# Six blocks of a matrix loaded at the beginning of a graph network's gated stage and not at its end

## The reference

```python
h = relu(layernorm(x)); x = x + L0(h)      # 10 propagation steps
h = relu(layernorm(x)); x = x + L1(h)      # the gated layer
h = relu(layernorm(x)); x = x + L2(h)      # two GCN convolutions with residuals
h = relu(layernorm(x)); x = x + L3(h)      # two weighted GCN convolutions, log_softmax

# L1, the gated layer
concat = concatenate([h[src], h[dst], edge_attr])
gated  = sigmoid(concat @ W_e + b_e) * softplus(concat @ W_n + b_n)
h_new  = segment_sum(gated, dst)
return h + h_new / clip(edge_count, 1)
```

## Time and profile before

| | |
|---|---|
| median of 3 runs | 2653.1 us |
| profiled execution | 2654.15 us, its span 2652.3 us |
| PE, DVE, ACT, POOL busy over the span | 85%, 62%, 50%, 42% |
| mean granted TensorE clock | 0.778 |
| gated stage, SP's first issue of it to that of the next stage | 1088.49 to 2148.15 us |
| DMA over the gated stage | some 110 to 120 GB/s in most slices |

### The profile page before, as it was taken

One profiled execution on the slowest core, in us unless ns is written; L12 is line 12 of the kernel. 1 busy time (PEld: TensorE's weight loads), 2 busy tenths in 40 slices (PEclk: granted clock), 3 DMA queues, 4 the chain that ended last, 5 costly groups with the idle time before them and its releaser, 6 DMA issues. The chain is left out here.

```text
span 2652.3 us, 55540 instructions
## 1 busy us (share of the span) xinstructions
PE 2257.7 (85%) x18268; PEld 2117.0 (80%) x18269; DVE 1637.7 (62%) x3208; ACT 1322.6 (50%) x2410; POOL 1109.4 (42%) x1222
## 2 busy tenths in 40 slices
PE   2999998699999999688888888788887768689998
PEld 1888888699999999587777777677777658689998
DVE  7998899764334335575666666656666564465465
ACT  1555555533333332265555555555555532267686
POOL 2666666300000000477777777777777701200000
PEclk6999999899999999655555555555555569879999
DMA  1444434300000001444444444444444551095281
GB/s 55 140 141 144 146 130 146 123 2 2 2 2 2 2 2 31 136 120 115 109 113 115 110 112 116 109 110 118 110 110 117 177 199 46 22 390 212 95 291 31
DMA packets 155980, 281.63 MB, mean 106 GB/s; under 512 B 73475, under 2 KB 123878, under 8 KB 150470
## 3 DMA queue, kind: packets, MB, share of 16 engines
q1 hardware_dynamic: 117158, 200.48, 23.3%
q0 software_dynamic: 38688, 79.28, 11.6%
HBM read 210.52 MB, written 69.15 MB: 105 GB/s over the span
## 5 line engine op out<-in xcount | busy, mean ns | idle before, releaser
L1245 POOL DMA_INDIRECT layer_R<-source_terms,layer_srcs x800 | 780.2, 975 | 243.7 <-issue 243.7
L1477 PE MATMUL layer_zp<-layer_right,layer_left 96*128 96x192 f32 x1342 | 476.9, 541 | 161.5 <-DVE layer_left L1264 158.4
L1477 PEld LDWEIGHTS layer_zp<-layer_right,layer_left 96*128 96x128 f32 x1342 | 409.6, 331 | 178.1 <-DVE layer_left L1264 167.4
L1008 PEld LDWEIGHTS layer_acc<-layer_U,graph_CT 128*128 128x128 f16 x6250 | 524.4, 97 | 32.0 <-ACT layer_U L937 22.5
L1008 PE MATMUL layer_acc<-layer_U,graph_CT 128*128 128x192 f16 (+1 forms) x6250 | 529.5, 246 | 23.4 <-ACT layer_U L937 21.5
L1498 PEld LDWEIGHTS layer_acc<-layer_hot,layer_G 128*98 128x98 f32 x1648 | 272.6, 274 | 108.1 <-DVE layer_aggT L1318 107.8
L1498 PE MATMUL layer_acc<-layer_hot,layer_G 128*98 128x32 f32 x1648 | 288.2, 344 | 45.8 <-DVE layer_aggT L1318 45.8
L2278 PE MATMUL layer_acc<-layer_V,layer_turn 128*128 128x96 f32 x2500 | 288.9, 278 | 0.6 <-issue 0.6
L2278 PEld LDWEIGHTS layer_acc<-layer_V,layer_turn 128*128 128x128 f32 x2500 | 287.0, 195 | 0.9 <-issue 0.9
L1423 ACT ACTIVATE layer_y<-layer_R 128x1152 f32<-128x1152 f32 x135 | 156.3, 1158 | 238.7 <-DVE layer_R L1292 238.7
L1292 DVE TENSOR_TENSOR layer_R<-layer_zp,layer_R 128x1152 f32<-128x1152 f32 x135 | 182.4, 1351 | 146.6 <-DMA layer_R<-source_terms,layer_srcs 146.4
(11 more groups left out here) (316 smaller groups left out, 3125.5 us busy)
## 6 DMA issues: line engine op xcount, KB each, us to landing
layer_ring<-W_blocks SPq DMA_DIRECT2D x41, 1600.0 KB, 7.6
W_blocks<-nodes_x SPq DMA_DIRECT2D x150, 200.0 KB, 1.9
layer_left<-in_attr SPq DMA_DIRECT2D x68, 384.0 KB
C_blocks<-build_Cblk SPq DMA_DIRECT2D x25, 800.0 KB, 3.4
layer_C<-C_blocks SPq DMA_DIRECT2D x19, 800.0 KB, 20.2
layer_R<-source_terms,layer_srcs POOLq DMA_INDIRECT x800
W_blocks<-build_Wtwo SPq DMA_DIRECT2D x50, 200.0 KB, 1.9
layer_rows<-target_rows SPq DMA_DIRECT2D x68, 96.0 KB
```

Of the source, the lines that this page charges most:

```text
L1008: return pe.matmul(acc[:, k % RING, 0:columns], CT[:, t, k * P:(k + 1) * P], pairs[:, cur, t, 0:columns], start=(t == 0), stop=(t == NT - 1))
L1245: nc.gpsimd.indirect_dma_start(R[:, i, u, :], None, P_d, bass.IndirectOffsetOnAxis(ap=at_u, axis=0)).then_inc(s_R[i], 16)
L1477: pe.matmul(out[u], left[:, i, u * P:(u + 1) * P], right[:, i, :], start=(u % 2 == 0), stop=False, skip_group_check=True)
```

## The change

The loop over the six blocks moves from behind the last pair of loads to behind the first one, ahead of the pair for steps 2 and 3. It gets a semaphore of its own, since `s_wa` is waited for early, at the value 144 of the nine weight loads, by DVE and PE. No instruction of another engine changes. Line numbers behind the first edit grow by one (L1193 is L1194 after).

```diff
@@ semaphores of gated_edges
+        s_first = m.sem("first_blocks_loaded")
@@ SP's program
             four_steps(sp, bases, counts, 0)
             loads(0, 0)
+            for j in range(FIRST):
+                sp.dma_start(C_first[:, j, :, :].rearrange("p k d -> p (k d)"), C_d[j, :, :]).then_inc(s_first, 16)
             with sp.Fori(0, NL - 1) as four:
                 loads(1, four * LONG + 2)
...
             loads(1, (NL - 1) * LONG + 2)
-            for j in range(FIRST):
-                sp.dma_start(C_first[:, j, :, :].rearrange("p k d -> p (k d)"), C_d[j, :, :]).then_inc(s_wa, 16)
             for i in range(NS - (NL - 1) * LONG):
                 more_loads(bases[i], counts[i])
-            sp.wait_ge(s_wa, 16 * (2 * LONG + 1 + FIRST))
+            sp.wait_ge(s_first, 16 * FIRST)
```

## The result

The changed kernel takes 2660.53 us (median of 11 runs, 2658.62 to 2662.39), the kernel before 2653.72 in the same comparison (11 runs, 2650.69 to 2655.84). The ratio is 1.0026, 95% interval 1.0017 to 1.0034: 6.8 us slower, where 3.1 were forecast. The median lies 1 us outside the range that was given and above the 2658.4 from which the prediction called the kernel slower; the interval of the ratio still takes in that mark (1.0020). The profiled execution took 2660.24 us, its span 2658.4 (before: 2654.15 and 2652.3).

A forecast was written before the change was run, and what follows sets the result against it. The prediction took POOL's unbroken line of 806 gathers to bound the gated stage. +5.6 us at its beginning and -2.5 at its end gave +3.1, so 2656.2 us from a median of 2653.1; range 2650.4 to 2659.5.

The forecast's parts named there:

- POOL is the bound and has no slack: In the gated stage POOL's 806 gathers wait only for their own issue, so any hold-up of POOL costs in full.
- What is gained at the end, 2.5 us: At the gated stage's end DVE's last additions come earlier without the burst there: 2.5 us gained.
- Which wait takes the place: At the stage's beginning DVE waits at L1264 for loads of steps 2 and 3, delaying logs(0) and POOL's step 4: 5.6 us.
- the 1.78 us that ACT covers: Between L1264 and L1297 DVE idled 1.78 us waiting for ACT, which covers that much of the lateness.
- The landing of the second pair, 1122.3: Loads for steps 2 and 3, queued behind the six blocks, land at about 1122.3, 16 us later than before.
- the first term: Cost at the gated stage's beginning: POOL's step 4 starts late, +5.6 us.
- the sum: +5.6 at the beginning and -2.5 at the end of the gated stage: +3.1 us.
- The starting point of 1106.3: Landing of the loads for steps 2 and 3 in the kernel before, read from the DMA share's fall: near 1106.3.
- Gathers up to 5 us late in the burst, and harmless: Gathers of steps 1 to 3 land up to 5 us late in the burst but are needed later: cost nothing.
- Rival A: Loads for steps 2 and 3 land by 1116.8, so only the end's 2.5 us remain: 2650.6; chance 0.16.
- Rival B: SP's full queue delays issuing loads for steps 2 and 3; they land at 1124.9, POOL 8.1 late: 2658.7; chance 0.13.
- Rival C: At the stage's end something else holds the last additions as long, so only +5.6 remains: 2658.7; chance 0.06.

The follow-up runs named there:

- the held run: The changed kernel, but SP issues the loads for steps 4 and 5 only when those for steps 2 and 3 have landed; 2657.11 us, ratio 1.0026.

## Why the prediction failed, step by step

- **POOL is the bound and has no slack:** right. In the profiles the gap on POOL is in the span one for one, and moving the burst to where POOL does not meet it gives about the 2.5 us and nothing else (2.9, 2.3 and 2.3 by the medians).
- **What is gained at the end, 2.5 us:** right, 2.6 in the profile, and 2.3 of it lost again with the burst at both ends.
- **Which wait takes the place:** right in each link: the second pair, DVE's L1264 (L1265 after), `logs(0)`, POOL's step 4, the 1.78 us that ACT covers, one gap and no other.
- **The landing of the second pair, 1122.3:** wrong, and this is the failed step. It was 1125.6, so the first term is 8.9 and not 5.6, and the sum 6.3 and not 3.1. With it 2653.1 + 6.3 = 2659.4 would have been forecast; the medians are 6.8 apart. I took the engines' work in mean share and let the pair land when the mean had done it. The blocks' mean end was about right: 1122.3 less (2.8 at most) / 0.70 for the pair is 1118.3, and their rate fell at 1117.6 + 0.4 = 1118.0. What was missing is that a transfer has landed only with its last arrival. In the changed kernel the blocks' last one came 3.9 us after the fall of the rate and the pair's another 3.5 us later, 7.4 us together where the sum had the pair's share of the work, 4.0. The time that the last few arrivals lag behind the mean was put at nothing, and no row was read for it. The starting point of 1106.3 had the same fault, by 0.7 us. The profile before had the warning in it: a pair took 6.0 us by that reading (6.8 by its last arrival) from first issue to landing, where its work on all 16 engines was put at 2.8 at most.
- **Gathers up to 5 us late in the burst, and harmless:** right. By their last arrivals those of steps 1, 2 and 3 came 2.7, 3.5 and 4.2 us later after their issue than in the kernel before, and no addition in these steps waits for them.
- **Rival A** (the cover holds): refuted for SP's queue by the 11.65 us, and true for ACT's queue, where the pair landed at 1113.93. The rule to issue early and wait late, which the prediction has beside this rival, holds for the transfer that was moved; the price was for those behind it.
- **Rival B** (SP's queue is full): its mechanism did not happen, SP issued all six in 3.02 us. Its price of 8.1 us was nearer than mine, because it counted a whole issue-to-landing time of 6.0 behind the end of the burst. That is luck: 2 of the 6.0 are issue, which the changed kernel had long behind it, and the blocks' last arrival was at 1121.9 and not at the 1118.9 from which B counts.
- **Rival C** (nothing at the end): refuted.
- **The range** ended at 2659.5, 0.8 above B and C. Its upper end took no account of a landing later than B's, though the mean share says nothing of the slowest engine.

Open: why one engine or several finish the burst later than the rest. The arrivals show that a few are late but not of which engine they are. Not all of the lag is an engine still moving blocks: their last packet ended 0.7 us before their last arrival in the run with the pair issued after them, and 1.05 us before it in the changed kernel. Open too is the scatter of POOL's own pace, 2 to 3.6 us over the stage from run to run.

Which place is best: behind the second pair the ratio is 0.9989, and its interval (0.9980 to 0.9998) excludes no change, though barely. The middle and ACT's queue point the same way with intervals that take in no change, so the runs do not rank the three. By the traces the middle has the most room: there DVE waits for no pair at all, where it waits 2.14 us for the third pair in the first and for the first and third in the last.

## What to carry to other kernels

When a large load is moved earlier on a queue, price what stands behind it and not the load: here a pair that was queued behind the burst landed 2.6 to 3.7 us after the last arrival of the burst, though it had been issued 8 us and more before that, and one issued only then landed 5.0 us after it. Ask then whether the engine that waits for it feeds the one without slack; the best place for a burst is one where the pacing engine is several steps ahead, or another queue, if the small loads have a few us to spare there too. And take a landing time from issue-to-landing times of like transfers, never from the mean share of the engines alone.

## What the runs showed of the hardware that was not expected

- After 4.9 MB in six transfers the last block landed about 2 us after the rate had fallen with nothing queued behind it, and 3.9 us after in the changed kernel, with a pair behind it. In the held run the mean share was 0.20 for three us while the last small transfer was still awaited.
- A pair of loads (528 KB in four transfers) took 5.8 us from first issue to use on nearly idle engines and 5.0 behind a landed burst; 2.0 of each are the issue.
- The same six blocks on ACT's queue kept the engines as full and made the second pair 7.5 us later, and the first one about 1 us late for DVE; behind them on SP's queue the pair took 22.0 us from first issue to landing, beside them 14.3.
